# A wait on the fourth attention maximum ahead of GpSimd's scatter of the previous batch's rows

## The reference, cut to what matters

```python
x = x + L1_attn(L1_cond(x, subject))        # attention: 8 heads, 64 wide, values 256 wide
x = x + L1_ffn(L1_cond2(x, profile))        # mixture: the 4 best of 32 experts for each token
# attention, for one sequence
attn = softmax(Q @ K.T)                     # per head, 512 x 512
out = sum over heads of attn @ V            # V of one head: 512 x 256
# mixture: each token goes to its 4 best experts, at most 512 places per expert
y[token] += swiglu(x[token], W1[e], W3[e], W2[e]) * weight[token, e]
```

## Time and profile before

| | us |
|---|---|
| three runs: lowest, median, highest | 4280.93, 4290.48, 4292.89 |
| the profiled execution, its own time | 4274.46 |
| its span | 4272.7 |
| PE busy (matmul) | 3415.9 (80%) |
| DVE busy | 2428.8 (57%) |
| ACT busy | 1474.4 (35%) |
| POOL (GpSimd) busy | 758.7 (18%) |

### The profile page before, as it was taken

The page is one execution under the profiler, slowest core; times in us unless marked ns, Lnnn a source line. Parts: engine busy times, 40 slices in busy tenths (PEclk is TensorE's granted clock), DMA queues, the critical chain, the costliest instruction groups (busy, mean ns, idle before and its releaser), DMA issues. The chain is left out here.

```text
span 4272.7 us, 35926 instructions
## 1 busy us (share of the span) xinstructions
PE 3415.9 (80%) x10447; PEld 1701.0 (40%) x10448; DVE 2428.8 (57%) x3026; ACT 1474.4 (35%) x2744; POOL 758.7 (18%) x646
## 2 busy tenths in 40 slices
PE   4788878787879785699699797979797979786991
PEld 1333323333333332366344343434343434344771
DVE  4699999999999999222133433333333333342335
ACT  1544535353535342133132323232323232322440
POOL 0000303030302113222100202020202020205551
PEclk9899989899989897799899898989898989897996
DMA  2122322232323242522200000000000010124447
GB/s 79 56 65 82 71 78 75 75 82 70 84 74 77 78 80 78 162 64 64 98 18 23 25 23 25 23 25 21 26 14 34 7 40 5 43 118 133 150 148 264
DMA packets 167475, 294.53 MB, mean 69 GB/s; under 512 B 33847, under 2 KB 90951, under 8 KB 166115
## 3 DMA queue, kind: packets, MB, share of 16 engines
q1 hardware_dynamic: 137202, 234.59, 19.2%
q0 software_dynamic: 26592, 55.83, 3.8%
q10 hardware_dynamic: 3600, 3.15, 0.2%
HBM read 200.58 MB, written 92.89 MB: 69 GB/s over the span
## 5 line engine op out<-in xcount | busy, mean ns | idle before, releaser
L399 POOL DMA_INDIRECT sorted<-rows,new_pl x192 | 256.9, 1338 | 2944.6 <-DVE new_pl L507 1482.4
L1123 PE MATMUL ps<-hs,ident 128*128 128x512 f32 x1024 | 556.8, 695 | 232.6 <-DVE hs L1231 232.6
L1225 DVE TENSOR_TENSOR_SCAN hs<-dA,hs 128x2048 f32<-128x2048 f32 x128 | 565.4, 4418 | 7.4 <-DVE hs L1217 0.9
L1820 PE MATMUL ps<-pT,V 128*128 128x512 f32 x1024 | 449.3, 593 | 7.0 <-DVE pT L1928 7.0
L1181 ACT ACTIVATE dA<-dl,w_An 128x511 f32<-128x511 f32 x512 | 326.1, 709 | 339.8 <-DVE hs L1225 338.1
L1123 PEld LDWEIGHTS ps<-hs,ident 128*128 128x128 f32 x1024 | 221.6, 223 | 555.1 <-DVE hs L1231 278.1
L1911 DVE TENSOR_REDUCE mx<-ps 128x4 f32<-128x2048 f32 x64 | 146.6, 2291 | 343.0 <-remote 183.6
L1217 DVE TENSOR_TENSOR hs<-u,bb 128x2048 f32<-128x2048 f32 x128 | 292.5, 2285 | 14.0 <-PE ps L1123 13.3
L1231 DVE TENSOR_TENSOR hs<-hs,cb 128x2048 f32<-128x2048 f32 x128 | 290.0, 2266 | 0.0
L405 POOL DMA_INDIRECT list<-new_slot,new_pl x192 | 271.9, 1416 | 88.9 <-issue 58.0
L1352 POOL DMA_INDIRECT slots<-og,idt x232 | 222.6, 959 | 336.2 <-DVE og L1452 207.4
(11 more groups left out here) (290 smaller groups left out, 5092.8 us busy)
## 6 DMA issues: line engine op xcount, KB each, us to landing
bb<-bcd SPq DMA_DIRECT2D x128, 256.0 KB
cb<-bcd SPq DMA_DIRECT2D x128, 256.0 KB
xg<-sorted SPq DMA_DIRECT2D x232, 128.0 KB, 2.0
slots<-zeros SPq DMA_DIRECT2D x136, 128.0 KB, 1.9
mb<-modd SPq DMA_DIRECT2D x64, 256.0 KB, 4.0
qrg<-slots SPq DMA_DIRECT2D x16, 1024.0 KB, 8.3
rg<-slots SPq DMA_DIRECT2D x36, 256.0 KB, 3.2
w_Lr<-in_Lora SPq DMA_DIRECT2D x9, 576.0 KB, 3.7
```

The lines of the kernel that those rows point to most:

```text
L399: pool.indirect_dma_start(M.sorted, bass.IndirectOffsetOnAxis(new_pl[:, t, i:i + 1], 0), v.rows[:, t, :], None).then_inc(M.listed, 16)
L1123: ins = pe.matmul(ps[:, j, :], ident[:, :], m.hs[:, N % 3, j, :], start=False, stop=(N % NS == NS - 1))
L1225: dve.tensor_tensor_scan(state, m.dA[:, N % 2].rearrange("p j t -> p (j t)"), state, 0.0, ALU.mult, ALU.add).then_inc(s_h, 1)
L1820: ins = pe.matmul(ps[:, 6 + j, :], V[:, m, h * D + j * P:h * D + (j + 1) * P], pT[:, i % 2, h % 2, m, :], start=(h == 0 and m == 0), stop= ...
```

## The change: one wait ahead of the sends

The diff adds one line. In `attention`, GpSimd first waits until `p_mx` has reached 4, that is until DVE has finished the fourth `maxima` of the batch in hand, and only then does what it did before. The order and number of the sends are the same. Batch 0, the last batch's routing and the first layer are not touched.

```diff
--- before.py
+++ after.py
@@ -1747,6 +1747,7 @@
                     @block.gpsimd
                     def _(pool):
                         if before is not None:
+                            pool.wait_ge(p_mx, 4)
                             send_rows(pool, M1, v, 0)
                             send_slots(pool, M1)
                             pool.wait_ge(M1.listed, b * (32 * TT * K1))
```

## The result

| | before | after |
|---|---|---|
| median of six runs each | 4287.5 us | 4301.9 us |
| runs | 4280.9 to 4292.9 | 4297.7 to 4305.0 |
| ratio, 95% interval | | 1.0029 (1.0019 to 1.0039) |
| profiled execution | 4274.5 us | 4297.7 us |
| span | 4272.7 us | 4295.9 us |

The account below looks back on a forecast made before the run. The prediction took a 25.4 us gap at the second maxima, caused by GpSimd's sends, as the loss in seven loop batches. 178 us removed less 14 us for the new place gave 164 us, so 4126 us; 8-in-10 range 4102 to 4312 us.

Parts of the forecast that it names:

- The gap comes from the sends: Second maxima of seven loop batches: GpSimd's sends cause the late start, 25.4 us a batch, 178 us in all.
- The wait itself: The added semaphore wait on GpSimd, idle 178.50 us before its first send, costs other engines 0 us.
- steps 0 to 3 as in batch 0: Loop batches' attention: without sends beside them, these steps run as in batch 0, removing 25.4 us of gap each.
- The end of the sends: End of the attention block: sends finish later but 28 us of slack are left, so 0 us cost.
- What the sends cost in their new place: Sends behind the fourth maxima: half of a 3.9 us wait, 2 us a batch, 14 us in seven.
- my other bound: Price of the sends' new place: nothing, as in the scan stage, where no such wait is listed.
- The range of the likeliest case: Whole kernel: new place costs 0 to 6.0 us a batch, 4112 to 4154 us; with the median's 10 us, 4102 to 4160.
- the gap moves and costs more: Rival, later attention steps: moved gap plus slowed TensorE clock, 3.4 us a batch, 24 us slower, 4314 us; chance 0.23.
- The term for the half clock: Later attention steps, in the dearer rival: half of 9.4 us at half clock shows on PE, 4.7 us a batch.
- at the same length: Rival: the gap moves with the sends and stays as long, so 4290.5 us; chance 0.13.
- Half a gap: Rival: only the wait's second half, 16.8 us, returns in the new place; 60 us saved, 4230 us; chance 0.12.
- not the sends: Rival: the loop's own code stalls, so the gap stays at the second maxima, 4290.5 us; chance 0.07.

Follow-up runs that it names:

- g2: The kernel before with the attention's sends left out (second experts read unsorted rows), on chip C: 4093.6 us against 4270.1 us.
- g1: The kernel before with each batch's 32 sends followed by 32 more into two tables nobody reads, on chip C: 4547.4 us against 4270.1 us.
- f1: The kernel before, unchanged, run on chip B: 4084.4 us beside 4098.1 us for the same kernel's 19 runs there.
- g3: The kernel before with only the 16 sends of numbers to the list, row sends left out, on chip C: 4119.8 us against 4270.1 us.
- g4: The kernel before with all 32 sends, four behind each of the eight maxima, on chip C: 4104.1 us against 4270.1 us.

## Why the prediction was wrong

**The gap comes from the sends: right.** With the sends left out it is gone on chip C (g2), and doubling them makes it 64.8 us long (g1). The size was right as well: 178 us were forecast as its cost in the kernel before, and without the sends chip C saved 4270.1 - 4093.6 = 176.5 us. Some of that is luck. The 25.4 us were taken from two batches against a batch 0 of 102.24 us. All seven windows average 128.6 us, and a loop batch without the gap takes 103.8 us (f1 and g2), so the gap costs 24.8 us a batch.

**The wait itself, 0 us, and steps 0 to 3 as in batch 0: right.** After the change DVE's second maxima follow 8.98 us after the first (2809.90 and 2818.88 in loop batch 3), and on chip B the wait changed nothing (0.9998).

**The end of the sends, 0 us: right.** The last one ends at 2881.53, 62 us before the window's end. They take their 40.6 us.

**What the sends cost in their new place, 2 us a batch: wrong, and this is the step that failed.** It was 29.7 us of waiting on DVE, and the window is 133.25 - 103.85 = 29.4 us longer than that of batch 0. I took the price from the experts' stage, where 16 sends left waits of 3.9 and 6.0 us, because its short steps were the nearest to the steady ones here. I then halved the row, since my other bound was zero. The row prices a run of 16 sends, 20 us long, whose late signals come through before its end, and g3 gives 3.3 to 3.7 us a batch for such a run in the attention, too. But the cost doesn't grow in proportion: 16 sends cost some 4 us, 32 cost 25 and 64 cost 65 on chip C. The kernel before had the first two of these points in view, 16 sends for some 4 us and 32 sends for 24.07. I read the difference as one of places when it was one of lengths. The zero of the scan stage, my other bound, says as little: its 8 + 8 sends follow each other every 1.97 and 3.06 us instead of every 1.26, so they are neither as many in a row nor as dense. The range of the likeliest case has a slip, too: 4154 us and 10 us for the median are 4164 us, not 4160.

**The rival "the gap moves and costs more": right in mechanism and nearly in size.** It gave 3.4 us a batch and 24 us; measured were 3.2 us and 23 us between the profiled executions, 14 us between the medians. Its bound was passed: the gap stayed longer than 20.7 us. The term for the half clock was too large at 4.7 us: the first values behind the gap and the two turns ahead of them lost 1.76 and 1.1 us, so 2.9 us, in a window whose clock is 0.69 where I took 0.61. With both in the sum the rival would have given 24.07 + 2.9 = 27.0 us, less than the 29.4 us measured: the wait itself was longer in the new place, which the rival didn't have. So its size came out near by two errors that cancel. It had 0.23 and "at the same length" 0.13; what spoke for them, that the waits end 3.4 and 4.8 us behind the last send, held in the new place, with 1.9 us on ACT and 4.8 us on DVE.

**Half a gap and "not the sends": wrong**, by the whole gap in step 4 and by g2.

The Trainium skill ("SBUF — State Buffer", section "Who interferes with whom") has GpSimd and DVE block each other at a shared pair of ports and says that PE and ACT never wait on anyone there. The sends here hardly grew: their median in the loop is 0.96 us in every trace that has them, with the gap and without. ACT and DVE both waited for turns that PE had done at 2857.60, so the rule doesn't explain the gap.

**What no step asked** is whether the gap belongs to the kernel at all. On four chips of the five named there is none: the medians of the kernel before are 4089 to 4102 us there, and there is nothing to remove.

## What to carry to other kernels

A stall that ends with another engine's run of transfers moves with them when they are moved, and breaks up when they are: four sends behind each of the eight maxima took 4104 us instead of 4270 on a chip with the gap (one run each) and the same time as the kernel before on two without (1.0002 and 0.9993). So this version was never behind by more than the noise, and 4% ahead where the gap is. When a row is to price an event somewhere else, match its length and count first and its surroundings second. And run the kernel on a second chip before work goes into a stall whose releaser the profile can't name.

## What the runs showed of the hardware

The same program takes 4270 to 4293 us in some jobs and 4084 to 4107 us in others, 4 to 5% apart, with sends of the same 0.96 us. One of five named chips had the gap. Chip C was met in one job only, so whether this lasts with a chip or comes and goes isn't shown.

The profiles of the chips with the gap differ in one more thing. Page part 6 of the kernel before, first as it was measured and then of f1, the same program on chip B:

```profile
bb<-bcd SPq DMA_DIRECT2D x128, 256.0 KB
cb<-bcd SPq DMA_DIRECT2D x128, 256.0 KB
```

```profile
bb<-bcd SPq DMA_DIRECT2D x128, 256.0 KB, 3.6
cb<-bcd SPq DMA_DIRECT2D x128, 256.0 KB, 3.3
```

The first has no time to landing for these loads. At least one of the two times is missing for the kernel after and for g1, g3 and g4 as well. g2 has both, and lacks that of the experts' loads. No time is missing in part 6 of any trace of chips A, B, D and E. In the two traces of the measurement and the four of chip C, and in them alone, some waits are put down to "remote", a few even in g2, which has no sends in the attention. So where signals come late, the record of landings has holes. Whether one causes the other isn't shown. Every run of the experiments comes with such a record (each has a granted clock), so nothing here tells whether the gap exists when nothing is recorded. That, why the first 16 us or so of a run do no harm, and whether SP's transfers would do the same, stay open.
